# A graph-attention kernel on one NeuronCore: first-layer adjacency tiles packed in groups of two or three, five of them unfolded, and GpSimd making both kinds of values at once

## The chip, the cores and the metric

One core of a Trainium2 chip. The metric is the device time of one execution in microseconds, as the median of three runs.

## The reference, cut to what matters

Four attention layers over a graph of 4096 nodes with 256 features and a dense 4096x4096 adjacency matrix of zeros and ones (int32). Layer 0 is:

```python
h = jnp.einsum('nf,hfd->hnd', x, W)                     # 4 heads of 64
e = jax.nn.leaky_relu(s_src[:, :, None] + s_dst[:, None, :], 0.01)
e = jnp.where(adj[None, :, :] == 0, -jnp.inf, e)
alpha = jax.nn.softmax(e, axis=-1)
out = jnp.einsum('hij,hjd->hid', alpha, h)
x = _layernorm(x + jax.nn.elu(out), axis=-1)
```

Layer 1 has the same form with slope 0.2; layers 2 and 3 use the same adjacency matrix with one head and more dense work. Only layer 0 reads the adjacency matrix from memory; the later ones use a packed copy.

## The kernel before, in words

The exponential of a leaky ReLU of a sum is, on either side of zero, a product of a factor of the row and one of the column. So a head's attention is two matrix products with masks of zeros and ones: the edges whose sum is positive (`pos`) times values of the first kind, and the other edges (`neg`) times values of the second kind. The masks are fp8, and each value is split into three bf16 parts of 65 columns (64 and the sum of weights), 195 columns a kind.

**Passes, groups, units.** A layer is four passes (one head each), a pass eight groups of 512 target rows, a group eight units of 512 source columns. `group` on TensorE (PE) runs 32 pairs of loads and matmuls a unit (lines 1432 and 1435), into four banks for one group and the other four for the next (`par`). For each unit ScalarE (ACT) makes `above` (line 1006, four operations of 128x512, BIG times the sum, clipped). VectorE (DVE) makes three operations in `masks`: `edge` from the packed words (line 1860), `pos` (1865) and `neg` (1868). There are two slots of each, so DVE may be two units ahead of PE, and ACT two ahead of DVE. During the units 1 to 4 of a group DVE also sums the three parts of the four banks of the group before (`sum_parts`, line 2027). GpSimd (POOL) then divides (`quotient`), and makes the values of the next pass (`values_of`, which calls `value_parts`, lines 537 to 558, once for each kind). Pass p's values are in slot p % 2.

**Loading and packing the adjacency matrix.** 32 tiles of 128x4096 are loaded on POOL's queue with a cast to bf16 (`load_adj`, line 602) into three staging buffers `adj_in`; tile t reuses the buffer of tile t - 3 and waits for its conversion. `convert` on DVE compares both halves with zero, weighs the second by 16 (lines 1778 and 1779), and adds them into one of two buffers `adj_bf` (line 1785): the tile is folded. `pack` on PE multiplies 16 blocks of the folded tile by diagonal matrices of powers of two (line 1373), which transposes and puts the bits of eight columns into a byte; `store_packed` copies the bank to `packed` (ACT line 977, or DVE line 1791). Eight tiles are packed before the first group, while layer 0's dense product runs; two of them (6 and 7) are packed at its end. The other 24 are packed inside the groups, in a bank that the group doesn't use and that was just summed.

**The order around the change** is written out by hand. `FRONT` lists the first ten groups as (pass, group). Groups of pass 0 and 1 are mixed, since each group has to find its rows of the matrix packed. Groups 0 to 7 of `FRONT` pack three tiles each. For tile n of a group DVE converts the first part at unit 2n and the second at unit 2n + 1 (counted from 0). PE packs it after unit 2n + 2. ACT copies the first and second after its `above` of units 4 and 6, the third after `above` of unit 0 of the next group; PE starts a group when all tiles of the group before are copied. POOL's queue holds, group by group: load orders, values of the second pass (two groups of them during each of the first four groups), the quotient of the group before. In the first group DVE also makes the values of pass 0, eight tiles at a time (lines 1888 to 1904), together with ACT's casts (line 990), and copies the tiles 6 and 7 after the masks of unit 1. After `FRONT` the rest of pass 1 runs in a loop of pairs of groups; POOL makes the values of pass 2 once the last group of pass 0 has ended (line 699).

## Time and profile before

| | |
|---|---|
| median of 3 runs | 3004.21 us (3003.21 to 3004.53) |
| profiled execution | 3004.37 us, of it span 3002.5 us |
| mean granted TensorE clock | 0.993 of full speed |
| TensorE matmul busy | 2906.4 us, 97% |
| VectorE, ScalarE, GpSimd busy | 2146.2, 1921.4 and 1193.9 us |

Busy times of engines overlap, so they don't add up to the span. A matmul's record is longer than the distance to the next one, since matmuls are pipelined. Distances between the starts of instructions on one engine say what an instruction costs there; its recorded duration is up to 0.1 us longer. The granted clock is a share of 2.4 GHz.

### The profile page before, as it was taken

The numbers are of one execution on the slowest core, as the hardware profiler recorded it, in microseconds if no ns is written. First come the engines' busy times: TensorE is split into PE (matmuls) and PEld (weight loads), VectorE is DVE, ScalarE is ACT, GpSimd is POOL, SyncE is SP. The second block draws the span as 40 slices with busy tenths as digits, with TensorE's granted clock in tenths as the row PEclk, the third lists the DMA queues.
The fourth block names the chain that finished last, engine by engine and source line by source line (L and its number), as shares of the span: only waits on it lengthen the run. The fifth ranks groups of instructions, "written<-read, shape, count | busy, mean of one in ns | idle before, by whom it ended". The sixth has DMA issues, their size and how long they took to land.

```text
span 3002.5 us, 64263 instructions
## 1 busy us (share of the span) xinstructions
PE 2906.4 (97%) x24148; PEld 2537.5 (85%) x24148; DVE 2146.2 (71%) x3920; ACT 1921.4 (64%) x3407; POOL 1193.9 (40%) x1591
## 2 busy tenths in 40 slices
PE   7789999999999999999999999999999999989999
PEld 6779999999989999999998878888788878755555
DVE  5999898888988888888886556666665666562245
ACT  4678899999988999999995545454455444430000
POOL 2572385642226565564221023333323333444222
PEclk9899999999999999999999999999999999999999
DMA  9555000000100000000010000000000000000001
GB/s 208 106 114 116 19 15 12 14 11 15 62 12 16 10 15 10 14 11 12 14 34 12 4 1 4 4 1 4 1 4 4 1 1 1 2 1 1 0 14 42
DMA packets 37301, 70.94 MB, mean 24 GB/s; under 512 B 9344, under 2 KB 22912, under 8 KB 33024
## 3 DMA queue, kind: packets, MB, share of 16 engines
q0 software_dynamic: 4608, 33.56, 5.8%
q1 hardware_dynamic: 30400, 34.49, 3.7%
q8 instruction: 107, 1.75, 0.2%
q10 hardware_dynamic: 2112, 0.52, 0.1%
q14 instruction: 74, 0.61, 0.1%
HBM read 97.73 MB, written 4.39 MB: 34 GB/s over the span
## 4 chain that ended last, share of the span: by engine, by line
PE 89%; DVE 6%; issue 2%; ACT 2%; POOL 1%; DMA 0%; DVEq 0%; ACTq 0%; POOLq 0%
PE bank L1432 20%; PE bank L1435 20%; PE bank L1489 16%; PE bank L1527 13%; PE bank L1438 11%; PE bank L1361 3%; PE bank L1516 2%; DVE rings L1865 2%; PE bank L1503 1%; ACT above L1006 1%; DVE rings L1860 1%; DVE rings L1868 1%; PE bank L1411 1%; PE bank L1324 1%; PE bank L1373 1%
## 5 line engine op out<-in xcount | busy, mean ns | idle before, releaser
L1432 PE MATMUL bank<-values,rings 128*128 128x195 bf16 x8192 | 1397.2, 249 | 51.7 <-DVE rings L1868 44.3
L1435 PE MATMUL bank<-values,rings 128*128 128x195 bf16 x8192 | 1397.0, 249 | 0.0
L1006 ACT ACTIVATE above<-srow,kpass 128x512 fp8e4<-128x512 f32 x2032 | 1280.7, 709 | 105.3 <-DVE rings L1868 95.9
L1432 PEld LDWEIGHTS bank<-values,rings 128*128 128x128 fp8e4 x8192 | 803.8, 98 | 68.4 <-issue 63.2
L1435 PEld LDWEIGHTS bank<-values,rings 128*128 128x128 fp8e4 x8192 | 803.8, 98 | 0.8
L1865 DVE TENSOR_TENSOR rings<-rings,above 128x512 uint32<-128x512 uint32 x512 | 389.9, 761 | 167.3 <-PE bank L1435 135.5
L1094 ACT ACTIVATE values<-srow,cmul 128x512 f32<-128x512 f32 x256 | 206.0, 815 | 411.5 <-PE bank L1527 410.5
L1868 DVE TENSOR_TENSOR rings<-rings 128x512 uint32<-128x512 uint32 x512 | 423.8, 828 | 17.3
L1527 PE MATMUL bank<-hv,values 128*128 128x257 f32 x1792 | 420.7, 380 | 0.0
L1527 PEld LDWEIGHTS bank<-hv,values 128*128 128x128 f32 x1792 | 335.8, 190 | 69.1 <-issue 25.2
L1438 PE MATMUL bank<-values,rings 128*128 128x390 bf16 x1920 | 319.3, 330 | 10.1 <-DVE values L1904 10.1
L1438 PEld LDWEIGHTS bank<-values,rings 128*128 128x128 fp8e4 x1920 | 188.4, 98 | 141.0 <-issue 13.1
L1860 DVE TENSOR_SCALAR rings<-packed 128x512 uint32 (+1 forms) x512 | 262.3, 512 | 2.0 <-ACT packed L977 1.9
L640 POOL TENSOR_TENSOR quot<-sums,cmul 128x260 f32<-128x260 f32 x64 | 47.1, 735 | 517.7 <-DVE sums L2027 398.7
L790 POOL TENSOR_SCALAR zrow<-zrow 128x1 f32<-128x1 f32 x128 | 46.7, 365 | 428.3 <-DVE zrow L2239 428.0
L1978 DVE SCALAR_TENSOR_TENSOR values<-values,cmul,rings 128x512 f32<-128x512 f32 x256 | 191.9, 757 | 34.6 <-ACT values L1094 34.2
L2098 DVE TENSOR_SCALAR rings<-packed 128x512 uint32 (+1 forms) x120 | 54.9, 458 | 199.7 <-PE bank L1438 199.6
L2027 DVE TENSOR_REDUCE sums<-bank 128x130 f32<-128x390 f32 x320 | 176.5, 554 | 3.5 <-PE bank L1411 1.7
L1489 PE MATMUL bank<-arena,above 128*128 128x256 f32 (+1 forms) x496 | 165.9, 482 | 0.8 <-ACT above L1149 0.8
L1489 PEld LDWEIGHTS bank<-arena,above 128*128 128x128 f32 x496 | 94.3, 190 | 52.8 <-issue 43.7
L1489 PE MATMUL bank<-quot,arena 128*128 128x256 f32 x512 | 118.3, 379 | 0.0
L793 POOL TENSOR_TENSOR zrow<-zrow,exponents 128x1 f32<-128x1 f32 x128 | 103.8, 811 | 19.5 <-POOL zrow L790 0.9
(235 smaller groups left out, 3457.6 us busy)
## 6 DMA issues: line engine op xcount, KB each, us to landing
arena<-in_adj_dram POOLq DMA_DIRECT2D x32, 1024.0 KB, 9.1
srow<-src_dram SPq DMA_DIRECT2D x69, 256.0 KB, 3.1
x<-in_x_dram SPq DMA_DIRECT2D x4, 1024.0 KB, 11.4
out_dram<-x SPq DMA_DIRECT2D x7, 512.0 KB, 2.9
arena<-in_L_gnn_fe_w_dram SPq DMA_DIRECT2D x2, 512.0 KB, 6.4
arena<-in_L_gnn_W_hz_dram SPq DMA_DIRECT2D x1, 1024.0 KB, 7.3
arena<-in_L_gnn_g_w_dram SPq DMA_DIRECT2D x1, 1024.0 KB, 10.9
weights<-in_L_gnn_W_dram SPq DMA_DIRECT2D x3, 256.0 KB, 3.5
```

The lines of the kernel that those rows point to most:

```text
L1006: last = act.activation(above[:, k % 2, q, :], srow[:, par, :], ACT.Relu, scale=BIG, bias=kpass[:, p % 2, k * Q + q:k * Q + q + 1], satura ...
L1094: act.activation(w2[:, m % DEPTH, :], srow[:, g % 2, :], ACT.Relu, scale=b_col[:, jt:jt + 1], bias=c_neg[:, jt:jt + 1]).then_inc(E.relu, 1)
L1432: pe.matmul(acc[:, 0:KW], pos[:, k % 2, q, :].bitcast(FP8)[:, rows], v[:, 0:KW], start=start, stop=final, skip_group_check=True)
L1435: last = pe.matmul(acc[:, KP:KP + KW], neg[:, k % 2, q, :].bitcast(FP8)[:, rows], v[:, KP:KP + KW], start=False, stop=final, skip_group_ch ...
L1438: last = pe.matmul(acc[:, 0:2 * KW], edge[:, k % 2, q, :].bitcast(FP8)[:, rows], v[:, 0:2 * KW], start=start, stop=final)
L1489: last = pe.matmul(dst, lhsT[k], rhs[k], start=(k == 0), stop=(k == len(lhsT) - 1))
L1527: last = pe.matmul(bank[it][:, 0:VW], w2[:, m % DEPTH, it * P:(it + 1) * P], hv[:, k * Q + q, :], start=(k == 0 and q == 0), stop=False)
L1860: dve.tensor_scalar(edge[:, r], words, shift[0], ONE, shift[1], ALU.bitwise_and).then_inc(s_dve, 1)
L1865: dve.tensor_tensor(pos[:, r], edge[:, r], above[:, r].bitcast(U32), ALU.bitwise_and).then_inc(s_dve, 1)
L1868: dve.tensor_tensor(neg[:, r], edge[:, r], pos[:, r], ALU.bitwise_xor).then_inc(s_sides, 1)
L1978: dve.scalar_tensor_tensor(out=w2[:, m % DEPTH, :], in0=w2[:, m % DEPTH, :], scalar=c_pos[:, jt:jt + 1], in1=edge[:, unit % 2, q, :].bitca ...
L2027: return dve.tensor_reduce(sums[:, slot, it, :, :], parts, AX.X, ALU.add)
```

## The change: what it does

- `FRONT` has twelve groups, with two more of the second pass, and (1, 0) one place earlier. `PACKS` says how many tiles each packs: 2, 3, 3, then eight times 2, then 0.
- Tiles 7, 8, 9, 10 and 13 are `UNFOLDED`: DVE compares the whole tile in one operation, adds nothing, and PE packs it straight from the staging buffer with 32 matmuls instead of 16. The load that reuses this buffer waits for PE's packing instead of DVE's conversion.
- Tables say where each step stands. A tile is converted from two units before its group to unit 4 of it; PE packs after units 1, 3 and 5 (4 and 6 in the first group); ACT copies after `above` of units 4, 6 and 7 (unit 7 and unit 0 of the next group for the first group's two). DVE copies tiles 6 and 7 after unit 3 of the first group instead of after unit 1.
- `both_kinds` on POOL makes both kinds with five operations of twice the width, in the passes of layers 0 and 1; the first group's calls keep `value_parts`.
- POOL makes the third pass's values one unit behind PE's last group of the first pass, mixed with the quotients of the second pass. PE starts the third pass's first two groups outside the loop and waits for the values unit by unit.

The diff, cut to its core:

```diff
-FRONT = [(0, 0), (0, 1), (0, 2), (0, 3), (0, 4), (1, 0), (0, 5), (1, 1), (0, 6), (0, 7)]
-PACKS = 3
+FRONT = [(0, 0), (0, 1), (0, 2), (0, 3), (1, 0), (0, 4), (1, 1), (0, 5), (1, 2), (0, 6), (1, 3), (0, 7)]
+PACKS = [2, 3, 3, 2, 2, 2, 2, 2, 2, 2, 2, 0]
+UNFOLDED = (7, 8, 9, 10, 13)
 VALUES_ORDER = [0, 3, 1, 2, 4, 5, 6, 7]
 VALUES_MADE = [max(VALUES_ORDER.index(j) for j in range(k + 1)) + 1 for k in range(BITS)]
 ...
-    return min(PACKED_FIRST + at * PACKS, T)
+    return PACKED_FIRST + sum(PACKS[:at])
 ...
+def pack_after(at, n):
+    return (4, 6)[n] if at == 0 else (1, 3, 5)[n]
+def store_after(at, n):
+    return ((0, 7), (1, 0))[n] if at == 0 else (at, (4, 6, 7)[n])
+def convert_after(at, n):
+    if at == 0:
+        return [(0, 3 + 2 * n)] * 2
+    if n == 0:
+        return [(0, 7)] * 2 if at == 1 else [(at - 1, 6), (at - 1, 7)]
+    return [(at, 0), (at, 2)] if n == 1 else [(at, 3), (at, 4)]
+STORE_AT = {store_after(at, n): (t, GT * (1 - at % 2) + n) for at in range(len(FRONT)) for n, t in enumerate(packs_of(at))}
+CONVERT_AT = {}
+for _at in range(len(FRONT)):
+    for _n, _t in enumerate(packs_of(_at)):
+        for _part, _when in enumerate(convert_after(_at, _n)):
+            CONVERT_AT.setdefault(_when, []).append((_t, _part))
 ...
+        def both_kinds(eng, chain, l, j0, p, slot):
+            big, rest = (vtmp_pool[:, i].rearrange("p (k n) c -> p k n c", k=2) for i in range(2))
+            e = emul[:, :, p, ds(j0, GT)].unsqueeze(3)
+            rows = h[:, ds(j0, GT), p * D:(p + 1) * D].unsqueeze(1)
+            kinds = values[:, slot, ds(j0, GT), :].rearrange("p n (k w) -> p k n w", k=2)
+            part = [kinds[:, :, :, i * C:(i + 1) * C] for i in range(PARTS)]
+            eng.tensor_copy(big[:, :, :, D:C], e)
+            eng.tensor_tensor(big[:, :, :, 0:D], rows.to_broadcast([P, 2, GT, D]), e.to_broadcast([P, 2, GT, D]),
+                              ALU.mult).then_inc(chain.sem, 1)
+            eng.wait_ge(chain.sem, chain.next())
+            eng.nop(nofuse=True)
+            eng.tensor_copy(part[0], big).then_inc(chain.sem, 1)
+            eng.wait_ge(chain.sem, chain.next())
+            eng.nop(nofuse=True)
+            eng.tensor_tensor(rest, big, part[0], ALU.subtract).then_inc(chain.sem, 1)
+            eng.wait_ge(chain.sem, chain.next())
+            eng.nop(nofuse=True)
+            eng.tensor_copy(part[1], rest).then_inc(chain.sem, 1)
+            eng.wait_ge(chain.sem, chain.next())
+            eng.nop(nofuse=True)
+            return eng.tensor_tensor(part[2], rest, part[1], ALU.subtract)
 ...
-                if t >= STAGED:
+                if t - STAGED in UNFOLDED:
+                    pool.wait_ge(s_packmm, t - STAGED + 1 + CREDIT)
+                elif t >= STAGED:
                     pool.wait_ge(s_adjbf, t - STAGED + 1)
                 pool.dma_start(adj_in[:, t % STAGED, :], A["adj"][t * P:(t + 1) * P, :])\
 ...
-                for kind in range(2):
-                    made = value_parts(pool, chain, vtmp, l, kind, g * GT, GT, p, p % 2)
+                if l < 3 and vtmp is vtmp_pool:
+                    made = both_kinds(pool, chain, l, g * GT, p, p % 2)
+                else:
+                    for kind in range(2):
+                        made = value_parts(pool, chain, vtmp, l, kind, g * GT, GT, p, p % 2)
                 made.then_inc(s_vals, 1)
 ...
             def front():
-                values = {at: VALUES_ORDER[2 * at:2 * at + 2] for at in range(NG // 2)}
+                values = {0: (0, 3), 1: (1, 2), 2: (4, 5), 3: (6, 7)}
                 load_adj(PACKED_FIRST + STAGED - 1)
                 for at in range(len(FRONT)):
                     vtmp = vtmp_pool if at else quot
                     loads = [t + STAGED for t in packs_of(at) if t + STAGED < T]
                     order = values.get(at, ())
-                    for t in loads[:1 if at < 2 else 2]:
+                    if at == 0:
+                        values_of(0, 1, order[0], vtmp)
+                    for t in loads[:1]:
                         load_adj(t)
                     if at < 2:
-                        values_of(0, 1, order[0], vtmp)
-                        for t in loads[1:2]:
-                            load_adj(t)
+                        values_of(0, 1, order[1 if at == 0 else 0], vtmp)
+                    for t in loads[1:2]:
+                        load_adj(t)
                     if at > 0:
                         quotient(0, *FRONT[at - 1], (at - 1) % 2, at - 1)
                     for t in loads[2:]:
                         load_adj(t)
-                    for v in order[1 if at < 2 else 0:]:
+                    for v in order[2 if at == 0 else 1 if at == 1 else 0:]:
 ...
-                pool.wait_ge(s_unit, len(FRONT) * BITS + CREDIT)
-                values_of(0, 2, 0)
+                def third(v):
+                    pool.wait_ge(s_unit, (len(FRONT) - 1) * BITS + v + 1 + CREDIT)
+                    values_of(0, 2, v)
+                third(0)
+                third(1)
                 quotient(0, *FRONT[-1], 1, len(FRONT) - 1)
-                values_of(0, 2, 1)
-                values_of(0, 2, 2)
-                for g in range(2, NG):
-                    if g + 1 < NG:
-                        values_of(0, 2, g + 1)
-                    quotient(0, 1, g, g % 2)
+                third(2)
+                quotient(0, 1, 4, 0)
+                third(3)
+                third(4)
+                quotient(0, 1, 5, 1)
+                third(5)
+                quotient(0, 1, 6, 0)
+                third(6)
+                third(7)
+                quotient(0, 1, 7, 1)
                 chain.settle()
             def row_factors(l):
 ...
-                per_group = VALUE_LINKS * 2 + links
+                per_group = VALUE_LINKS * (1 if l < 3 else 2) + links
                 if l < 2:
                     row_factors(l)
 ...
-                other = GT * (1 - par)
-                if k in (4, 6) and k // 2 - 2 < len(packs_of(at)):
-                    store_packed(packs_of(at)[k // 2 - 2], other + k // 2 - 2)
-                if k == 0 and at > 0 and len(packs_of(at - 1)) == PACKS:
-                    store_packed(packs_of(at - 1)[PACKS - 1], GT * par + PACKS - 1)
+            def stores_behind(at, k):
+                if (at, k) in STORE_AT:
+                    store_packed(*STORE_AT[at, k])
             def store_packed(t, b):
-                act.wait_ge(s_packmm, t * 2 + (2 + CREDIT))
+                act.wait_ge(s_packmm, t + 1 + CREDIT)
                 act.activation(packed_bytes[:, :, t * P:(t + 1) * P],
                                bank[b][:, :].rearrange("p (q n) -> p q n", q=Q), ACT.Copy).then_inc(s_packed, 1)
 ...
                     if k >= UNITS_AHEAD:
                         above_of(k + 1, (2, 3))
+                        if at is not None:
+                            stores_behind(at, k + 1)
                 row_factors(l)
             def scores_of(l, p):
 ...
-            def pack_half(t, half, b):
+            def pack(t, b):
+                raw = t in UNFOLDED
+                tile = adj_in[:, t % STAGED, :] if raw else adj_bf[:, t % 2, :]
+                slices = BITS if raw else BITS // 2
                 pe.wait_ge(s_adjbf, t + 1)
-                for k in range(half * (BITS // 4), (half + 1) * (BITS // 4)):
+                for k in range(slices):
                     for q in range(Q):
                         j = k * Q + q
-                        last = pe.matmul(bank[b][:, q * P:(q + 1) * P], adj_bf[:, t % 2, j * P:(j + 1) * P],
+                        last = pe.matmul(bank[b][:, q * P:(q + 1) * P], tile[:, j * P:(j + 1) * P],
                                          powers[:, k, :], start=(k == 0 and q == 0),
-                                         stop=(k == BITS // 2 - 1 and q == Q - 1), skip_group_check=True)
+                                         stop=(k == slices - 1 and q == Q - 1), skip_group_check=True)
                 last.then_inc(s_packmm, 1)
-            def pack(t):
+            def pack_first(t):
                 pe.wait_ge(s_packed, t + 1)
-                for half in range(2):
-                    pack_half(t, half, 6 + t % 2)
+                pack(t, 6 + t % 2)
             def first_row(l):
 ...
-                    if k in (2, 4, 6) and k <= 2 * len(packs):
-                        n = k // 2 - 1
-                        if at == 0:
-                            pe.wait_ge(s_src, 1)
-                            pe.wait_ge(s_packed, PACKED_FIRST + CREDIT)
-                        else:
-                            pe.wait_ge(s_banksum, PACKS * (at - 1) + n + 1)
-                        for half in range(2):
-                            pack_half(packs[n], half, GT * (1 - par) + n)
+                    for n, t in enumerate(packs):
+                        if pack_after(at, n) == k:
+                            if at == 0:
+                                pe.wait_ge(s_src, 1)
+                                pe.wait_ge(s_packed, PACKED_FIRST + CREDIT)
+                            else:
+                                pe.wait_ge(s_banksum, (GT - 1) * (at - 1) + n + 1)
+                            pack(t, GT * (1 - par) + n)
             def one_pass(l, p):
-                begun = p == 0 or (l == 0 and p == 1)
-                if p > 0:
+                begun = 2 if l == 0 and p == 1 else 1 if p == 0 or (l == 0 and p == 2) else 0
+                if l == 0 and p == 2:
+                    for par in range(2):
+                        pe.wait_ge(s_sums, p * NG + par + 1)
+                        group(0, 0, par, p * NG + par, made=None if par else [NG + k + 1 for k in range(BITS)])
 ...
+                elif p > 0:
                     pe.wait_ge(s_vals, p * NG + values_before(l))
                 if p == 0:
                     for par in range(2):
                         pe.wait_ge(s_sums, TURN[l] * SUMS + par + 1)
                         group(l, 0, par, par, first=(par == 0))
                 final = l == 3 and p == PASSES[3] - 1
-                with pe.Fori(1 if begun else 0, NG // 2 - final) as gg:
+                with pe.Fori(begun, NG // 2 - final) as gg:
                     for par in range(2):
                         pe.wait_ge(s_sums, gg * 2 + (p * NG + TURN[l] * SUMS + par + 1))
 ...
-            def convert(t, half):
+            def convert(t, part):
                 raw = adj_in[:, t % STAGED, :]
-                if half == 0:
+                if part == 0:
                     dve.wait_ge(s_adj[t % STAGED], (t // STAGED + 1) * 16)
+                    if t in UNFOLDED:
+                        dve.tensor_scalar(raw, raw, 0.0, None, ALU.is_gt).then_inc(s_adjbf, 1)
+                        return
                     dve.tensor_scalar(raw[:, 0:N // 2], raw[:, 0:N // 2], 0.0, None, ALU.is_gt)
                     dve.tensor_scalar(raw[:, N // 2:], raw[:, N // 2:], 0.0, float(2 ** (BITS // 2)),
                                       ALU.is_gt, ALU.mult).then_inc(s_adjone, 1)
-                    return
-                if t >= 2:
-                    dve.wait_ge(s_packmm, t * 2 - 2 + CREDIT)
-                dve.wait_ge(s_adjone, t + 1)
-                dve.tensor_tensor(adj_bf[:, t % 2, :], raw[:, 0:N // 2], raw[:, N // 2:], ALU.add)\
-                    .then_inc(s_adjbf, 1)
+                elif t not in UNFOLDED:
+                    if t >= 2:
+                        dve.wait_ge(s_packmm, t - 1 + CREDIT)
+                    dve.wait_ge(s_adjone, t + 1 - len([u for u in UNFOLDED if u < t]))
+                    dve.tensor_tensor(adj_bf[:, t % 2, :], raw[:, 0:N // 2], raw[:, N // 2:], ALU.add)\
+                        .then_inc(s_adjbf, 1)
             def store_packed(t, b):
-                dve.wait_ge(s_packmm, t * 2 + (2 + CREDIT))
+                dve.wait_ge(s_packmm, t + 1 + CREDIT)
                 dve.tensor_copy(packed_bytes[:, :, t * P:(t + 1) * P],
                                 bank[b][:, :].rearrange("p (q n) -> p q n", q=Q)).then_inc(s_packed, 1)
 ...
                                 pass
-                            if l == 0:
-                                store_packed(PACKED_WOVEN, 6 + PACKED_WOVEN % 2)
                     else:
                         made = masks(l, unit, k, words)
 ...
                     if front is not None:
-                        if l == 0 and first and k == 0:
-                            store_packed(PACKED_WOVEN + 1, 6 + (PACKED_WOVEN + 1) % 2)
-                        if k < 2 * len(packs_of(g)):
-                            convert(packs_of(g)[k // 2], k % 2)
+                        if first and k == 3:
+                            for t in range(PACKED_WOVEN, PACKED_FIRST):
+                                store_packed(t, 6 + t % 2)
+                        for t, part in CONVERT_AT.get((g, k), ()):
+                            convert(t, part)
                     if fold is not None and k >= GT:
                         fold_weights(fold, k - GT)
 ...
                               fold=1 if at == len(FRONT) - 1 else None)
-                    one_pass(0, 1, 1)
+                    one_pass(0, 1, 2)
                     one_pass(0, 2)
                     final_pass(0)
                     return
```

## Rows read from the trace of the kernel before

**Rows 1.** The page: busy us and share of the span.

```profile
PE 2906.4 (97%) x24148; PEld 2537.5 (85%) x24148; DVE 2146.2 (71%) x3920; ACT 1921.4 (64%) x3407; POOL 1193.9 (40%) x1591
```

**Rows 2.** Busy times by stretch: the first sixteen groups, with PE's granted clock.

```profile
core 0: us, PE busy (x) PEld busy (x) DVE busy (x) ACT busy (x) POOL busy (x), PEclk, DMA share, GB/s
69.50:116.80 47.30, 34.49 (x328) 32.61 (x329) 42.65 (x65) 29.42 (x51) 23.91 (x33) 0.78 0.50 97
116.80:148.10 31.30, 25.48 (x313) 24.58 (x311) 30.66 (x38) 22.39 (x37) 24.15 (x32) 1.00 0.58 111
148.10:176.90 28.80, 25.27 (x309) 24.23 (x306) 28.16 (x38) 22.30 (x36) 17.14 (x24) 1.00 0.62 119
176.90:209.20 32.30, 25.35 (x304) 24.05 (x304) 29.87 (x39) 22.17 (x36) 25.21 (x35) 1.00 0.54 107
209.20:237.05 27.85, 24.30 (x296) 23.44 (x297) 25.40 (x38) 20.90 (x34) 12.67 (x15) 1.00 0.62 124
237.05:317.45 80.40, 74.61 (x915) 72.35 (x913) 71.88 (x110) 65.43 (x106) 19.21 (x21) 1.00 0.48 96
317.45:382.90 65.45, 65.22 (x770) 64.32 (x768) 56.58 (x94) 60.99 (x98) 28.32 (x37) 1.00 0.04 14
382.90:426.80 43.90, 43.71 (x519) 43.15 (x517) 40.09 (x57) 40.93 (x65) 39.15 (x53) 1.00 0.04 13
426.80:491.00 64.20, 64.20 (x764) 63.88 (x763) 54.76 (x86) 59.83 (x97) 37.49 (x48) 1.00 0.04 13
```

**Rows 3.** PE in the first group: waits in total; its third unit; a packing.

```profile
PE bank L1432 <- DVE rings L1868: 12.8, 3, 6.0
...
82.94 0.32 PE L1432 MATMUL bank<-values,rings 128*128 128x195 bf16 x1 [5.96 <-DVE rings L1868]
...
258.42 0.89 PE bank L1373 x16
```

**Rows 4.** DVE in order of time, after the cut at 237.05: start, duration.

```profile
237.05 0.56 DVE L2027 TENSOR_REDUCE sums<-bank 128x130 f32<-128x390 f32 x1
237.53 1.22 DVE L1785 TENSOR_TENSOR arena<-arena 128x2048 bf16<-128x2048 bf16 x1
238.66 0.42 DVE L1860 TENSOR_SCALAR rings<-packed 128x512 uint32<-128x512 uint32 x1
...
240.45 0.56 DVE L2027 TENSOR_REDUCE sums<-bank 128x130 f32<-128x390 f32 x1
```

**Rows 5.** DVE in order of time, in the first group.

```profile
71.21 1.27 DVE L1791 CAST packed<-bank 128x512 uint8<-128x512 f32 x2
...
75.09 0.17 DVE L1888 COPY vtmp_pool<-emul 128x8 f32<-128x8 f32 x1
...
88.10 0.17 DVE L1888 COPY vtmp_pool<-emul 128x8 f32<-128x8 f32 x1
...
94.09 0.68 DVE L1778 TENSOR_SCALAR arena<-arena 128x2048 bf16<-128x2048 bf16 x1
94.69 0.68 DVE L1779 TENSOR_SCALAR arena<-arena 128x2048 bf16<-128x2048 bf16 x1
```

**Rows 6.** Who waited for whom, 237 to 263.8: us, times, longest.

```profile
ACT packed L977 <- PE bank L1373: 3.7, 3, 1.2
...
DVE rings L1865 <- ACT above L1006: 1.0, 1, 1.0
```

**Rows 7.** POOL: load orders around a call; wide operations elsewhere (mean ns).

```profile
119.02 0.59 POOL L602 DMA_DIRECT2D arena<-in_adj_dram  x1 [10.00 <-DVE arena L1785]
...
129.53 0.59 POOL L602 DMA_DIRECT2D arena<-in_adj_dram  x1
...
L822 POOL TENSOR_TENSOR values<-rings,values 128x512 f32<-128x512 f32 x16 | 23.2, 1453 | 21.6 <-ACT rings L1141 20.5
...
L829 POOL TENSOR_SCALAR values<-values 128x512 f32<-128x512 f32 x16 | 9.9, 617 | 119.5 <-ACT values L1163 119.4
```

**Rows 8.** The adjacency tiles' loads.

```profile
DMA to landing us min/median/max: 7.9/9.1/19.4
```

More of the change, by code:

```diff
@@ L964, in above_ahead @@
                     last.then_inc(s_above, 1)
-            def stores_behind(at, par, k):
-                other = GT * (1 - par)
-                if k in (4, 6) and k // 2 - 2 < len(packs_of(at)):
-                    store_packed(packs_of(at)[k // 2 - 2], other + k // 2 - 2)
-                if k == 0 and at > 0 and len(packs_of(at - 1)) == PACKS:
-                    store_packed(packs_of(at - 1)[PACKS - 1], GT * par + PACKS - 1)
+            def stores_behind(at, k):
+                if (at, k) in STORE_AT:
+                    store_packed(*STORE_AT[at, k])
             def store_packed(t, b):
-                act.wait_ge(s_packmm, t * 2 + (2 + CREDIT))
+                act.wait_ge(s_packmm, t + 1 + CREDIT)
                 act.activation(packed_bytes[:, :, t * P:(t + 1) * P],
@@ L1019, in group @@
                         if at is not None:
-                            stores_behind(at, par, k)
+                            stores_behind(at, k)
                         if elu is not None and k == 2:
@@ L1030, in group @@
                         if at is not None:
-                            stores_behind(at, par, k)
+                            stores_behind(at, k)
                     next(one)
@@ L1069, in attention @@
                         continue
-                    with act.Fori(1 if l == 0 and p == 1 else 0, NG // 2) as gg:
+                    with act.Fori(2 if l == 0 and p == 1 else 0, NG // 2) as gg:
                         for par in range(2):
@@ L1726, in _ @@
                                 pe.wait_ge(s_srow[0], 16)
-                            pack(q - 1)
+                            pack_first(q - 1)
                         if l < 2 and q == ROW_AT:
@@ L1732, in _ @@
                         for t in range(PACKED_WOVEN, PACKED_FIRST):
-                            pack(t)
+                            pack_first(t)
                 if l != 2:
```

## The prediction

> **What bounds the kernel now.** I read the page's busy times first: TensorE (PE) is busy 97% of the span [rows 1], so only places where it stands still, runs at the low clock or does extra work can change the time. Then I cut the first layer's attention into its groups of eight units, each cut where VectorE (DVE) sums the first bank of the group before [rows 2]. The reader is to see three regimes. The last three of the sixteen groups, with nothing to pack, take 64.2 us with PE at 100%, 21.4 each: PE bound. The three at 237.05, which pack three tiles each, take 26.8 each. The first takes 47.3, the next four 31.3, 28.8, 32.3 and 27.85, with DVE busy for nearly all of the second and third. All sixteen fill 421.5 us. Sixteen times 21.4 and 24 packings of 0.89 us [rows 3] make 364, so some 57 us are lost here, the most that any schedule could find.
>
> Why are they lost? Distances between starts price DVE's steps [rows 4]: a bank's sum 0.48, the addition that folds a tile 1.13, a unit's shift and two masks 1.79. A compare over half a tile is 0.60 [rows 5], so a tile costs DVE 0.60 + 0.60 + 1.13 = 2.33. A group is 8 x 1.79 + 4 x 0.48 = 16.2, and with three tiles 23.2. The groups at 116.8 and 148.1 take 31.3 and 28.8 with DVE idle for 0.6 in each (gaps between instructions): the rest is stretch, which goes with GpSimd's (POOL's) work beside it. Per us of POOL's busy time it is (31.3 - 23.2)/24.15 = 0.34 and (28.8 - 23.2)/17.14 = 0.33; in the next two, less 1.8 us each of further idle time, (30.5 - 23.2)/25.21 = 0.29 and (26.0 - 23.2)/12.67 = 0.22 [rows 2]. In the 26.8 us groups a second cause shows: ScalarE (ACT) waits up to 1.2 us for each packing, its above() then comes late, and DVE waits 1.0 for that [rows 6].
>
> The first group adds a third: PE waits three times for masks, 12.8 us in all, up to 6.0 [rows 3], and the granted clock of this stretch is 0.78 against 1.00 later [rows 2], so a part of it runs at 1.2 GHz instead of 2.4, behind these waits.
>
> **The change, part by part.**
> (1) First group. From 71.21 to 75.09 DVE copies two packed tiles and converts tile 8 [rows 5]; both move behind the fourth mask. Tile 7's addition, 1.13 before and about 0.9 net of a wait for ACT's cast, goes. So PE's third unit starts at 82.9 [rows 3] less 3.9 less 0.9, 78.1. Values, shift and masks of one unit take DVE from 88.10 to 94.09, 6.0 us [rows 5]; the copies were 1.2 of the 3.9. The fifth unit then starts at 78.1 + 1.8 (fourth mask) + 0.4 (stretch) + 1.2 (copies) + 1.15 (tile 8 unfolded: one compare of twice the width of one of 0.60, no addition) + 6.0 = 88.6, the seventh at 88.6 + 1.8 + 1.15 + 6.0 = 97.6. Then 2.7 for it (21.4/8), 1.8 for tile 9's packing (32 matmuls instead of 16), 2.7 for the eighth: 103 to 105; I take 104.8, and the cut 2.2 later, 107. PE waits some 5 us in front of the fifth unit and runs slowly behind it, which lies beside DVE's next 9 us and costs nothing. The group takes 37.5; gain 9.8.
> (2) POOL makes both kinds of values at once: five operations on 520 elements instead of ten on 260. A call runs between two orders of a load, from 119.61 to 129.53, 9.9 us [rows 7]. No row has the wide form. A product of 128x512 took 1.45, a one-input operation of 128x512 0.62 [rows 7]: three of the first, two of the second, 0.5 for the small copy and 0.6 of links are 6.7; the other bound is 9.9, if width costs its full price. I take 7.3, near the low end, since the nearest rows are of nearly this size, with 0.6 for casts that write at a stride. POOL is off the path; what counts is DVE's stretch.
> (3) Groups 2 to 5. DVE's bare work: 16.2 with tiles 11 and 12 and the single compare of 13, 22.0; with 14, 15 and, moved forward, 16, 23.2; with two tiles 20.9 and 20.9. A quotient is 19.21/3 [rows 2] less two load orders of 0.59 [rows 7], 5.2; I use 5.4. POOL has two calls and a quotient, 20, then by its queue 16.7, 20 and 10. With a stretch of 0.33, 0.33, 0.3 and 0.3 the groups are 28.6, 28.7, 26.9 and 23.9, sum 108.1 against 120.25: gain 12.1. PE's own work is 25.3 at most (three packings, one unfolded), so it does not take over.
> (4) Groups 6 to 11, two tiles each: DVE 20.9 + 1.6 of stretch, ACT at most its present 65.43/3 = 21.8 [rows 2], PE 21.4 + 1.8 = 23.2. PE becomes the bound. Packing now follows units 2 and 4 instead of 3 and 5, the copies still follow ACT's above() of units 5 and 7: one or two units more between them, over the 1.2 us of [rows 6]. I take 23.4. Three of these replace 80.4 (gain 10.2), three replace 65.45 (loss 4.75).
> (5) Groups 12 and 13: 42.8 instead of 43.9 [rows 2], gain 1.1. The third pass's values are now made while the second pass ends, each unit's overwritten one unit behind PE. By the queue the last is ready 8 us into the third pass's first group and read 18.7 us in (7 x 2.7): nothing. Without that cover it would be a call, 7.3.
> (6) An unfolded tile holds its staging buffer until PE has packed it, so tiles 11, 12, 13 and 16 are ordered later, and what is queued behind them on POOL with them, 14 and 15 too. A load lands in 9.1 us, 7.9 to 19.4 [rows 8]. By the times of (1) and 3.6 us a unit after that, tile 11 is ordered at 95 and wanted at 102, tile 12 at 103 and 112, tile 14 at 121 and 130. DVE's lead on PE of up to a unit hides about 2.5 us of each. I charge 2 us in all, of 0 to 30. The score rows on the sync queue are ordered a group ahead as before and are covered.
> (7) The later passes and layers: PE is at 100% at 426.8 with POOL busy 37.49 of 64.2 us [rows 2], so the wide operations are worth nothing there; bounds -3 and +3.
>
> Sum: 9.8 + 12.1 + 10.2 - 4.75 + 1.1 - 2 = 26.4 us. The profiled execution took 3004.4 (span 3002.5 and 1.9 around it), the median is 3004.2, so 2978.
>
> The stretch in [rows 2] goes with POOL's busy time. The Trainium skill (GPSIMD Engine Reference, Key points) says that GpSimd shares its SBUF interfaces with VectorE, against instructions in a 2-port mode or with two SBUF inputs, which the two masks are; by that rule the traffic counts, and the elements that POOL moves stay the same. Rival C below is this case.
>
> **Rivals.**
> A: slower. The loads of (6) come late, at DVE's compares in groups 2 and 3. For: some took 19.4 [rows 8], and POOL's queue is strict. Against: most take 9.1. If tiles 11 to 16 all come at 19.4, six times 10.3 less 2.5 covered is 47, less the 28.4 found before the charge: 3023. It decides from 4.7 us of uncovered delay for each of the six.
> B: the groups with two tiles stay above PE's work, since DVE's conversions still lie between two masks: 25.0 instead of 23.4, for eight groups 13 us: 2991. For: the 1.0 us wait of DVE for ACT [rows 6]. Against: DVE's bare work falls to 20.9.
> C: the stretch goes with elements. Then it stays at the 23.8 us of groups 2 to 5 (8.1 + 5.6 + 7.3 + 2.8) instead of my 21.1: 2981.
> D: more than forecast. Groups 4 and 5 reach PE's 23.4 (4.0 less), the tight loads cost nothing (2 less), and groups 2 and 3 lose 4 of the stretch: 2968. For: in the three groups at 237.05 stretch is small. Against: POOL has still 20 us of work beside them.
> E: nothing changes, since the lost time belongs to packing 24 tiles wherever they stand. Against: groups without packing run at PE's speed [rows 2]. 3004.
>
> **How the numbers follow.** My forecast, with C in its spread, 0.62; B 0.17; D 0.11; A 0.06; E 0.04. The likeliest runs from 2973 to 2984. The range takes in B and D nearly whole, 2967 to 2992, and leaves out A, E and the tails, about 0.15. A measurement of this kernel can tell 0.2%, 6 us. Slower holds most of A, 0.05; the same E and a little of the rest, 0.05; faster 0.90.
>
> **What would show it.** Right: the first group under 40 us, with one long PE wait, in front of the fifth unit; ACT's waits for packing nearly gone; groups with two tiles at 23.2 to 23.6 with PE at 100%; POOL's calls at about 7.3 us; the end of the sixteenth group at about 465 instead of 491. Wrong: DVE waiting for loads inside the groups, stretched masks that make PE wait in the later passes, or groups of 25 us in the middle.

## The result and the profile after

The changed kernel takes 3033.15 us (median of 4 runs, 3032.6 to 3034.07) against 3004.37 on the same chip: ratio 1.0096, 95% interval 1.0079 to 1.0114. It is slower by 28.8 us. The forecast was 2978, range 2967 to 2992.

Page of the changed kernel: busy times, the chain that ended last, TensorE's main line with its idle time before it, and VectorE's two masks and shift.

```profile
PE 2913.7 (96%) x24228; PEld 2536.8 (84%) x24228; DVE 2185.1 (72%) x3910; ACT 1918.6 (63%) x3407; POOL 1062.4 (35%) x1315
...
PE 84%; DVE 10%; issue 3%; ACT 1%; POOL 1%; DMA 1%; DVEq 0%; ACTq 0%; POOLq 0%
...
L1500 PE MATMUL bank<-values,rings 128*128 128x195 bf16 x8192 | 1398.1, 248 | 74.9 <-DVE rings L1942 64.6
...
L1939 DVE TENSOR_TENSOR rings<-rings,above 128x512 uint32<-128x512 uint32 x512 | 406.9, 795 | 157.8 <-PE bank L1503 129.3
...
L1942 DVE TENSOR_TENSOR rings<-rings 128x512 uint32<-128x512 uint32 x512 | 438.2, 856 | 17.3
...
L1934 DVE TENSOR_SCALAR rings<-packed 128x512 uint32 (+1 forms) x512 | 276.2, 540 | 0.1
```

GpSimd is busy for 131.5 us less than in [rows 1] and VectorE for 39 us more, although it has fewer instructions. TensorE's idle time in front of its main line is 74.9 us; before, the same line had 51.7:

```profile
L1432 PE MATMUL bank<-values,rings 128*128 128x195 bf16 x8192 | 1397.2, 249 | 51.7 <-DVE rings L1868 44.3
```

The groups of the first layer, cut as in [rows 2], with its columns.

```profile
69.00:108.40 39.40, 31.39 (x352) 30.22 (x349) 38.76 (x59) 29.51 (x51) 23.04 (x32) 0.91 0.37 70
108.40:138.75 30.35, 25.72 (x320) 24.97 (x320) 29.25 (x37) 21.80 (x35) 18.56 (x20) 1.00 0.77 146
138.75:170.40 31.65, 25.96 (x323) 24.96 (x320) 31.10 (x39) 21.81 (x35) 20.30 (x21) 1.00 0.60 112
170.40:202.45 32.05, 27.08 (x288) 25.90 (x288) 28.26 (x35) 21.45 (x34) 17.68 (x19) 0.89 0.43 82
202.45:226.05 23.60, 23.60 (x291) 23.25 (x288) 21.51 (x36) 21.21 (x34) 5.86 (x7) 1.00 0.59 110
226.05:343.85 117.80, 117.68 (x1443) 116.25 (x1440) 107.15 (x172) 106.29 (x170) 25.59 (x33) 1.00 0.49 93
343.85:366.35 22.50, 22.47 (x279) 22.30 (x277) 17.85 (x31) 21.14 (x34) 4.17 (x5) 1.00 0.06 16
366.35:393.70 27.35, 23.41 (x271) 22.37 (x268) 25.03 (x37) 20.53 (x33) 16.57 (x17) 1.00 0.03 11
393.70:415.95 22.25, 21.09 (x249) 20.92 (x250) 19.61 (x30) 19.65 (x32) 10.55 (x11) 1.00 0.05 14
415.95:485.60 69.65, 65.91 (x776) 64.69 (x774) 61.83 (x85) 60.82 (x98) 40.21 (x43) 1.00 0.04 12
```

At the end of group 11 the kernel is 16.5 us ahead of before (366.35 against 382.90). Then group 12 takes 27.35, and the last three take 69.65 where [rows 2] has 64.2, with TensorE no longer at 100%. The sixteenth ends at 485.6, only 5.4 ahead. So the new schedule works, and something eats its gain in the groups where GpSimd has calls.

What a call does, in the second layer, where nothing is packed: GpSimd and VectorE in order of time.

```profile
978.39 0.82 POOL L600 CAST values<-vtmp_pool 128x520 f32 x1 [0.22 <-POOL vtmp_pool L596]
979.36 1.39 POOL L603 TENSOR_TENSOR vtmp_pool<-vtmp_pool,values 128x520 f32<-128x520 f32 x1 [0.15 <-POOL values L600]
980.96 0.62 POOL L606 CAST values<-vtmp_pool 128x520 f32 x1 [0.22 <-POOL vtmp_pool L603]
981.82 1.30 POOL L609 TENSOR_TENSOR values<-vtmp_pool,values 128x520 f32 x1 [0.24 <-POOL values L606]
```

```profile
979.67 1.36 DVE L1934 TENSOR_SCALAR rings<-packed 128x512 uint32 x1
981.24 0.88 DVE L1939 TENSOR_TENSOR rings<-rings,above 128x512 uint32<-128x512 uint32 x1 [0.21 <-DVE rings L1934]
982.16 1.51 DVE L1942 TENSOR_TENSOR rings<-rings 128x512 uint32<-128x512 uint32 x1
983.60 0.41 DVE L1934 TENSOR_SCALAR rings<-packed 128x512 uint32 x1
```

What follows on TensorE, and a wide product with a sum and a shift beside it, at the end of the second pass:

```profile
983.82 0.24 PE L1500 MATMUL bank<-values,rings 128*128 128x195 bf16 x1 [1.01 <-DVE rings L1942]
```

```profile
485.31 1.39 POOL L603 TENSOR_TENSOR vtmp_pool<-vtmp_pool,values 128x520 f32<-128x520 f32 x1
```

```profile
485.63 0.55 DVE L2101 TENSOR_REDUCE sums<-bank 128x130 f32<-128x390 f32 x1
486.11 0.88 DVE L1934 TENSOR_SCALAR rings<-packed 128x512 uint32 x1
```

The shift of 0.41 us takes 1.36 and the mask of 0.69 takes 1.51, each while one wide product runs (979.36 to 980.75, 981.82 to 983.12). The unit from 979.67 to 983.60 takes 3.93 us; TensorE needs 2.70 (86.30/32, below), and it waits 1.01 for the mask. The Trainium skill (SBUF — State Buffer, Who interferes with whom) says that of a GpSimd instruction and a VectorE instruction in a 2-port mode (or with two SBUF inputs, where GpSimd's reads SBUF) whichever issues first holds the shared ports for its whole length and the other fully blocks, and that a reduction on VectorE never contends. The trace agrees in both: the shift and the mask end 0.28 and 0.55 us after the product beside them, so each does most of its work behind it, and the sum takes its 0.55 us inside a product, as in [rows 4].

### The profile page after: what moved, and what is told of

Same layout as the page of the kernel before. It is cut to its first block, busy times and chain, and to the rows that moved or that the text cites. A ratio compares the mean times of both kernels' runs of the same rounds, so it can differ in the third digit from the quotient of the medians.

```text
span 3031.7 us, 63637 instructions
## 1 busy us (share of the span) xinstructions
PE 2913.7 (96%) x24228; PEld 2536.8 (84%) x24228; DVE 2185.1 (72%) x3910; ACT 1918.6 (63%) x3407; POOL 1062.4 (35%) x1315
## 4 chain that ended last, share of the span: by engine, by line
PE 84%; DVE 10%; issue 3%; ACT 1%; POOL 1%; DMA 1%; DVEq 0%; ACTq 0%; POOLq 0%
PE bank L1500 18%; PE bank L1503 18%; PE bank L1560 16%; PE bank L1598 13%; PE bank L1506 11%; DVE rings L1939 3%; PE bank L1427 3%; DVE rings L1942 2%; DVE rings L1934 2%; PE bank L1587 2%; PE bank L1574 1%; PE bank L1442 1%; PE bank L1479 1%; PE bank L1390 1%; ACT above L1070 1%
## 5 line engine op out<-in xcount | busy, mean ns | idle before, releaser
L1500 PE MATMUL bank<-values,rings 128*128 128x195 bf16 x8192 | 1398.1, 248 | 74.9 <-DVE rings L1942 64.6
L1939 DVE TENSOR_TENSOR rings<-rings,above 128x512 uint32<-128x512 uint32 x512 | 406.9, 795 | 157.8 <-PE bank L1503 129.3
L1942 DVE TENSOR_TENSOR rings<-rings 128x512 uint32<-128x512 uint32 x512 | 438.2, 856 | 17.3
L1934 DVE TENSOR_SCALAR rings<-packed 128x512 uint32 (+1 forms) x512 | 276.2, 540 | 0.1
L2172 DVE TENSOR_SCALAR rings<-packed 128x512 uint32 (+1 forms) x120 | 54.7, 456 | 199.9 <-PE bank L1506 199.8
## 6 DMA issues: line engine op xcount, KB each, us to landing
x<-in_x_dram SPq DMA_DIRECT2D x4, 1024.0 KB, 11.7
```

Source lines behind the costliest of these rows:

```text
L1500: pe.matmul(acc[:, 0:KW], pos[:, k % 2, q, :].bitcast(FP8)[:, rows], v[:, 0:KW], start=start, stop=final, skip_group_check=True)
L1934: dve.tensor_scalar(edge[:, r], words, shift[0], ONE, shift[1], ALU.bitwise_and).then_inc(s_dve, 1)
L1939: dve.tensor_tensor(pos[:, r], edge[:, r], above[:, r].bitcast(U32), ALU.bitwise_and).then_inc(s_dve, 1)
L1942: dve.tensor_tensor(neg[:, r], edge[:, r], pos[:, r], ALU.bitwise_xor).then_inc(s_sides, 1)
```

## Experiments

All on one core, beside the kernel before (medians of 3004.4 to 3005.3 us). "e2" and the like are short names; times are medians.

**Which part costs.** e1 puts `both_kinds` alone into the kernel before; e2 is the changed kernel with `value_parts` everywhere; e3 is e2 with the wide form only where the second pass's values are made; e4 keeps the combined form, two tiles at a time, so ten operations of 260 elements.

```diff
-                if l < 3 and vtmp is vtmp_pool:
+                if l == 0 and p == 1 and vtmp is vtmp_pool:     # e3
...
+                    for half in range(2):                       # e4
+                        made = both_kinds(pool, chain, l, g * GT, p, p % 2, half)
```

> The kernel before with nothing changed but GpSimd's wide calls (both kinds at once). Theory W (a wide call presses as much stretch on VectorE into two thirds of the time, so its masks fall behind the matmuls in the later passes): slower than before by 40 to 50 us, 3045 to 3055, with groups of about 22.7 instead of 21.4 us in the passes that make values. Rival S (the new order of the first passes sets the loss): within 5 us of 3004.

> The changed kernel with the narrow calls of before everywhere. Theory W: 2978 to 2990, that is before less the 16 us that the profile after shows gained up to the twelfth group, and some more where wide calls stretched the groups 2 to 4. Rival S: 3025 to 3035, since the order is kept.

> The changed kernel with wide calls for the second pass's values alone (six calls in the first groups), narrow calls elsewhere. Theory W: 2983 to 2992, with 2 to 6 us more than with narrow calls everywhere, because six calls cost about 1 us each. Rival S: 3025 to 3035.

> The changed kernel, with both kinds in one call as there, but over two tiles at a time: ten operations of 260 elements with the wide form's strides and broadcasts. Theory W (the width of an operation matters): like the narrow calls, 2978 to 2990. Rival L (the layout of the combined form is what hurts VectorE): like the changed kernel, 3025 to 3035.

Measured: e1 3048.97 us (ratio 1.015, interval 1.0133 to 1.0167); e2 2982.02 (0.9926, 0.991 to 0.9943); e3 2989.27 (0.9949, 0.9933 to 0.9966); e4 2981.96 (0.9926, 0.9909 to 0.9943). The schedule is worth 23 us, and the wide operations cost 44 on the old schedule and 51 on the new. The combined form isn't to blame, only its width. All four lie in the ranges of theory W, though e3 lies 7.3 us above e2 and not 2 to 6. In the front the wide form costs 7.3 us (e3 less e2), elsewhere the remaining 44.

**Which operations, and width or density.** e5 keeps the three products wide and splits the casts; e6 the reverse; e7 leaves all wide and puts four memsets of 520 elements on one partition, each with a link, around the casts; e8 uses quarter operations of 130 elements; e13 splits every operation into two of 260 without a link between.

```diff
-            eng.tensor_copy(part[0], big).then_inc(chain.sem, 1)
+            eng.tensor_copy(part[0][:, 0], big[:, 0])                        # e5, e13
+            eng.tensor_copy(part[0][:, 1], big[:, 1]).then_inc(chain.sem, 1)
...
+            def pad(i):                                                      # e7
+                eng.memset(vtmp_pool[0:1, i].rearrange("p n c -> p (n c)"), 0.0).then_inc(chain.sem, 1)
...
+                        for half in range(2):                                # e8
+                            made = value_parts(pool, chain, vtmp, l, kind, g * GT + 2 * half, 2, p, p % 2)
```

> The kernel after, with its three wide products per call kept at 520 elements and its two wide casts per call made as four casts of 260. The last four runs showed that the 520-element operations cost some 50 us; this tells which kind of them does. Theory P (the products count: two-input operations of 1.3 us each, during whose whole length a VectorE operation of one input was seen held): little is gained, 3020 to 3033. Rival K (the casts count: 0.6 to 0.8 us each, writing bf16 with a stride): 2982 to 2990. If each operation counts in proportion to its length, products being 3.9 of 5.4 us: about 3019.

> The mirror of the run before: products of 260 elements (six per call, in pairs without a link between), casts of 520. Theory P (products): 2982 to 2992. Rival K (casts): 3015 to 3033. In proportion to length: about 2996. A pair of products follows without a pause, so if what counts is how long VectorE is held by an unbroken stretch of GpSimd's traffic and not by one instruction, this run stays near 3025 too although each product is short.

> The wide calls of the kernel after, unchanged, but with four fillers in each: a memset of 520 elements on one partition, with a link of its own, around each of the two casts. The call should grow from 6.4 to 9 or 10 us with the same wide operations in it, as long as the ten narrow ones take. Theory D (density: the masks of two or three units in a row are stretched by 0.5 us per us, and VectorE's lead is used up; spread over a call 1.5 times as long the lead lasts): 2985 to 3000. Rival I (a single instruction's length: the stretch is done by the 1.3 us products, wherever they stand): 3020 to 3035. If the fillers themselves hold VectorE: above 3033.

> The kernel after, with values made in twenty operations of 130 elements (one kind of two tiles at a time) everywhere that GpSimd makes them behind the first group. Theory W (narrower is gentler): the later passes stay free of waits of TensorE for masks as with 260 elements, so at most 5 us come off there, but the calls grow to 13 us or more and their stretch in groups 2 to 5 of the front grows or stays: 2976 to 2985. Rival F (every GpSimd instruction adds a fixed share of traffic and stall of its own): VectorE is stretched more in all, 2990 to 3010.

> The kernel after with every wide operation of a call split into two of 260 elements, one for each kind, that follow each other without a link, so a call has four links as the wide one has, and no instruction wider than the narrow form's. Theory U (the unbroken stretch between two links is what holds VectorE): VectorE is busy 77 us in four groups of the second layer as with wide products or wide casts alone, 2990 to 3000 in all. Rival I (the width of an instruction): 73 us and 2982 to 2986, as with ten operations and eight links.

Measured: e5 3003.62 us (0.9997, 0.9987 to 1.0007), e6 2995.3 (0.9962, 0.9948 to 0.9976), e7 3010.28 (1.002, 1.001 to 1.0029), e8 3015.72 (1.0036, 1.0024 to 1.0049), e13 2983.67 (0.9931, 0.9915 to 0.9948). To see why, the same four groups of the second layer, which hold equal work in every kernel (1025 to 1027 matmuls, four calls, four quotients; only e8's stretch catches some more of GpSimd's work, 123 instructions where four calls and quotients have 116). One stretch each, of after, e2 and e13:

```profile
970.78:1061.17 90.39, 86.90 (x1027) 85.95 (x1026) 78.09 (x113) 80.25 (x129) 40.60 (x44) 1.00 0.05 12
```

```profile
943.46:1029.68 86.22, 86.22 (x1027) 86.15 (x1026) 73.08 (x113) 80.81 (x129) 52.99 (x68) 1.00 0.04 12
```

```profile
943.41:1029.64 86.23, 86.23 (x1027) 86.15 (x1026) 73.93 (x114) 81.28 (x129) 51.27 (x64) 1.00 0.04 12
```

| kernel | one call, us | four groups, us | VectorE busy, us | whole kernel, us |
|---|---|---|---|---|
| before | 10.7 | 86.30 | 72.81 | 3004 |
| after: all wide | 6.3 | 90.39 | 78.09 | 3033 |
| e7: all wide, spread | 9.1 | 86.82 | 77.49 | 3010 |
| e5: products wide | 7.3 | 86.77 | 77.57 | 3004 |
| e6: casts wide | 7.9 | 86.24 | 77.03 | 2995 |
| e13: narrow pairs | 9.1 | 86.23 | 73.93 | 2984 |
| e2: narrow | 10.0 | 86.22 | 73.08 | 2982 |
| e8: quarter | about 15 | 86.06 | 72.66 | 3016 |

(The call of e8 is 4/3 of three of its quarter rounds, which take 11.14 us from 979.29 to 990.43.) Two effects are to be seen. Wide operations hold VectorE longer in all: 78.09 less 73.08 is 1.25 us a call. The whole traces show how: in the changed kernel 85 second masks overlap a product of a call and take 1.26 us in the mean, in e2 162 do and take 0.92, against 0.69 for one with no GpSimd work beside it. Half as many are held, each for more than twice as long. Narrow pairs add nearly nothing, so this goes with the width of an instruction and not with the unbroken stretch between two links (theory U falls). And the extra 1.1 us of e7, 1.1 of e5 and 1.0 of e6 cost TensorE 0.15 us a group or less, the 1.25 in a call of 6.3 us cost 1.04: what VectorE loses seems to count once it comes faster than the two slots of lead can take. So both theories of e7 had a part; it falls between them. (Its fillers are GpSimd work too and may hold VectorE themselves.) Wide products and wide casts cost 21.6 and 13.3 us alone and 51 together; e6's five runs spread from 2990.5 to 2997.0, so its figure is good to a few us. Of e5's two theories neither range holds 3003.6, and e6 is at the value in proportion to length, 2996. Why wide casts hold VectorE as much as wide products is not settled.

These four groups aren't where e5, e6 and e7 lose most. In the traces they are 22.2, 14.2 and 26.3 us behind e2 at the end, and 11.7, 11.2 and 13.3 of that by the cut after the sixteenth group, where calls stand beside conversions or one behind another. What limits them there no run separates.

e8 is slower than either of its theories allowed (2976 to 2985, 2990 to 3010). It loses nothing in these groups, but GpSimd becomes late elsewhere. One stretch of it, at the start of the third pass, and its waits there (us in total, times, longest):

```profile
486.57:529.32 42.75, 27.05 (x260) 25.64 (x259) 18.95 (x29) 20.29 (x32) 35.36 (x81) 0.76 0.02 7
```

```profile
PE bank L1502 <- POOL values L586: 15.7, 2, 10.6
```

That group takes 21 us more than 21.5, and the granted clock falls to 0.76 behind the waits. Groups 2 to 5 are longer too: 126.2 us (109.01 to 235.16) against 110.1 in e2. 260 elements lie between two losses.

**The schedule's parts**, each undone on e2: no tile unfolded (e9), packing one unit later (e10), the third pass's values after the first pass's last group (e11), more tiles unfolded (e12, e14).

```diff
-UNFOLDED = (7, 8, 9, 10, 13)
+UNFOLDED = ()                                             # e9
+UNFOLDED = (7, 8, 9, 10, 12, 13, 15, 16)                  # e12
+UNFOLDED = (7, 8, 9, 10, 11, 12, 13, 14, 15, 16, 17)      # e14
...
-    return (4, 6)[n] if at == 0 else (1, 3, 5)[n]
+    return (4, 6)[n] if at == 0 else (2, 4, 6)[n]         # e10
...
-                    pool.wait_ge(s_unit, (len(FRONT) - 1) * BITS + v + 1 + CREDIT)
+                    pool.wait_ge(s_unit, len(FRONT) * BITS + CREDIT)     # e11
```

> The schedule of the change with narrow calls (2982.0 us) and no tile unfolded: the tiles 7, 8, 9, 10 and 13 are folded again. VectorE then does 1.13 us more for each, TensorE 0.89 less. Theory V (the first five groups are bound by VectorE): 7, 8 and 9 cost the first group about 3.4 us, 10 and 13 the next two 1.1 each, so 5 to 6 us more: 2987 to 2989. Rival L (the unfolded tiles hold their staging buffers, so their loads were costing time): the two cancel or it is faster, 2978 to 2984.

> The schedule of the change with narrow calls, but TensorE packs after units 2, 4 and 6 again instead of 1, 3 and 5, while ScalarE copies after its above() of units 4, 6 and 7 as in the change. Theory S (packing and copying apart is what brings the two-tile groups to TensorE's own 23.4 us): ScalarE waits up to 1.2 us for each packing again and the eight two-tile groups go from 23.55 to 24.5 or more, 2989 to 2994. Rival N (with two tiles instead of three VectorE has slack enough, and ScalarE's wait is hidden): 2980 to 2984.

> The schedule of the change with narrow calls, but GpSimd makes the third pass's values only after the last group of the first pass has ended, in the order of the change. Eight calls of 9.9 us and four quotients of 5.2 after the end of that group at about 380 end at 480, and the third pass reads its first values at about 466 and its eighth at 485. Theory C (covered unit by unit): 2981 to 2984. Rival Q (the calls stand in front of the quotients, so sums are freed late and the second pass's last groups wait for GpSimd): 2987 to 2995.

> The schedule of the change with narrow calls and three more tiles unfolded, 12, 15 and 16. The groups 2 to 4 take 29.4, 28.8 and 27.7 us with TensorE's own work at 25.3 or less, so each 1.13 us less on VectorE should count in full and each 0.89 more on TensorE not at all. Theory V: 3 us faster, 2978 to 2980. Rival L (a buffer held until the packing makes the third load after it late): 2983 to 2992.

> The schedule of the change with narrow calls and the tiles 7 to 17 all unfolded (before: 7 to 10 and 13; then 12, 15 and 16 as well, which gave 3.1 us). Tiles 11, 14 and 17 come off VectorE too, 1.13 us each, and TensorE does 0.89 more for each: group 2 then has three unfolded packings, 21.4 + 5.3 = 26.7 us of TensorE, and takes 27.7 already, so little is left: theory V: 2977 to 2979.5. Rival L (every load in a row waits for a packing, so loads come late): 2982 or more.

Measured: e9 2988.92 us (0.9949, 0.9931 to 0.9967), e10 2985.6 (0.9936, 0.9918 to 0.9954), e11 2981.69 (0.9924, 0.9906 to 0.9941), e12 2978.95 (0.9915, 0.9898 to 0.9933), e14 2981.47 (0.9925, 0.9908 to 0.9942).

e9: the five unfolded tiles are worth 7 us, but at another place than expected. Its first group and the next three:

```profile
68.90:115.62 46.72, 31.99 (x322) 29.97 (x320) 45.76 (x67) 30.60 (x53) 28.84 (x42) 0.81 0.53 100
115.62:200.25 84.63, 73.70 (x896) 71.29 (x896) 82.26 (x109) 64.74 (x104) 60.16 (x78) 1.00 0.51 99
```

The first group ends 7.2 us later than in e2 (115.62 against 108.46), with a longest wait of TensorE for masks of 8.4 us; the next three take 1.4 less than e2's 86.0. Tile 10 is converted in the first group too, so four additions, 4.5 us, fall there, and not the expected three; the other 2.7 aren't accounted for.

e10: ScalarE waits for packing again, in the two-tile groups from 222.8 to 339.7 and in groups 2 to 4:

```profile
ACT packed L1038 <- PE bank L1439: 11.5, 10, 1.5
...
ACT packed L1038 <- PE bank L1439: 17.2, 8, 3.9
```

The five two-tile groups take 116.84, not longer than e2's 117.78, so there the waits are hidden; groups 2 to 4 take 89.8 instead of 86.0. Theory S had the place wrong. In groups 2 to 4 VectorE also waits 4.6 us for loads (0.2 in e2), whose buffers the later packing holds longer; which of the two waits costs the 3.8 us isn't told apart. e11: theory C holds, making the values later costs nothing. e12: theory V holds, 3.1 us, and by the cuts groups 2 to 4 take 83.3 instead of 86.0. e14 runs from 2978.56 to 2982.86, between its two theories, and unfolding three more gives nothing that shows. The intervals of e2, e10, e11, e12 and e14 overlap, so differences of 3 us among them rest on the cuts of single traces.

e12 beats both kernels: 25 us under before and 54 under after.

## Why the prediction was wrong

**The step that failed is (7)**, "PE is at 100% at 426.8 with POOL busy 37.49 of 64.2 us [rows 2], so the wide operations are worth nothing there; bounds -3 and +3". It costs 40 us of the 55 that the forecast missed. The three groups that it reads take 69.65 us instead of 64.2, 5.4 more. From the cut after the sixteenth group to the end of the span before has 3002.5 - 491.0 = 2511.5 us, e2 2981.0 - 469.1 = 2511.9 and after 3031.7 - 485.6 = 2546.1, 34.6 more. The step took TensorE at 100% to mean that VectorE has slack for whatever the change does. There was slack, in a call too, but little. In a call of before the first masks start 2.7 us apart, each after a wait for TensorE:

```profile
974.12 0.69 DVE L1865 TENSOR_TENSOR rings<-rings,above 128x512 uint32<-128x512 uint32 x1 [0.39 <-PE bank L1435]
...
976.81 0.69 DVE L1865 TENSOR_TENSOR rings<-rings,above 128x512 uint32<-128x512 uint32 x1 [0.59 <-PE bank L1435]
...
979.51 0.69 DVE L1865 TENSOR_TENSOR rings<-rings,above 128x512 uint32<-128x512 uint32 x1 [0.39 <-PE bank L1435]
```

Some 0.2 us of each wait is there without TensorE too (the 0.21 behind the shift at 981.24 above), so 0.2 to 0.4 a unit was free. The wide call takes 1.25 us more of VectorE within 6.3 us, little more than two units. In the four groups of the table VectorE waited for TensorE before, and TensorE never for VectorE; after, TensorE waits once a call, 3.5 of the 4.1 us that they grew (before, then after):

```profile
DVE rings L1865 <- PE bank L1435: 11.6, 28, 0.6
```

```profile
PE bank L1500 <- DVE rings L1942: 3.5, 4, 1.0
```

**The price behind it** was the assumption of (3) that stretch goes with GpSimd's busy time. Shorter calls stretched VectorE more, 5.0 us over four calls. Rival C let the stretch keep its sum, and only in groups 2 to 5; it didn't have that the width of an instruction counts. The prediction read out of the Trainium skill (GPSIMD Engine Reference, Key points) that the traffic counts; that section says only which VectorE instructions GpSimd disturbs. With equal traffic VectorE was busy 73.08 us with narrow operations and 78.09 with wide ones.

Point by point:
- (1) First group: 8.4 us gained of 9.8. One long wait was forecast in front of the fifth unit; there are two, 7.5 us in all: 3.6 in front of the third unit and 3.9 in front of the fifth. The third starts at 78.0 and the fifth at 89.1 (78.1 and 88.6 forecast), so the order of events was right.
- (2) A call: 6.3 us, forecast 7.3, between load orders 9.9 before. The low bound of 6.7 was not low enough.
- (3) Groups 2 to 5: 108.1 forecast, 110.1 with narrow calls (e2), 117.65 as changed. The wide form was counted as saving stretch here; it costs 7.5.
- (4) Groups 6 to 11: 140.4 forecast (six times 23.4), 140.3 measured. TensorE is the bound, as argued. Rival B is false.
- (5) Groups 12 and 13: 42.8 forecast, 45.65 in e2, 49.6 as changed. Group 12 also folds weights on VectorE, and two calls follow each other from its second half on (373.1 to 392.0 in e2), which the step didn't price. The cover for the third pass's values is right (e11).
- (6) Loads: 2 us charged, VectorE waited 0.6 in groups 2 to 4. Rival A, the one for slower, is false: slower came from elsewhere.
- The schedule without wide calls: 26.4 us forecast, 23 measured. By the cuts the misses are 1.5 in (1), 2.0 in (3), 2.9 in (5), and the 2 of (6) back.

Waits of the changed kernel, first group, then groups 2 to 4 (us in total, times, longest), beside [rows 3] and [rows 6]:

```profile
PE bank L1500 <- DVE rings L1942: 7.5, 2, 3.9
...
ACT packed L1041 <- PE bank L1442: 1.6, 1, 1.6
```

```profile
PE bank L1500 <- DVE rings L1942: 15.6, 10, 3.6
...
ACT packed L1041 <- PE bank L1442: 3.0, 3, 1.3
DVE arena L1852 <- DMA arena<-in_adj_dram: 0.6, 1, 0.6
```

TensorE waits for masks ten times in groups 2 to 4; ScalarE hardly waits for packing and VectorE hardly for loads.

## What to carry to other kernels

An engine at 100% with a feeder at 84% is safe only if the feeder keeps up in each stretch as long as its buffers' lead: price a change of the neighbour's work per unit there, not over the pass. On two engines that hold each other up, don't merge operations to shorten a call that isn't on the path; here 260 elements per GpSimd instruction was best, 520 held VectorE and 130 made GpSimd late. Split a change into its parts before judging it: this one held a gain of 23 us and a loss of 51.

## What the runs showed of the hardware that was not expected

- GpSimd doing the same elements in half the instructions kept VectorE busy for 1.25 us more a call (78.09 against 73.08 us in four groups), though its own busy time fell from 52.99 to 40.60.
- The effect needs the wide instruction, not wide traffic without a pause: pairs of narrow ones back to back gave 73.93.
- For TensorE the parts don't add up: wide products 21.6 us, wide casts 13.3, both 51.
- A one-input shift of 128x512 was held as long (0.41 to 1.36 us) as a mask with two inputs (0.69 to 1.51), each until about the end of the wide product beside it.
- VectorE's sums out of the banks kept their time beside a call: 0.55 us inside a wide product that held the next shift from 0.42 to 0.88.
